# Input gate times cell gate on GpSimd in the last slot of a graph and LSTM kernel

## What is computed

```python
def _L1_gnn_ref(x, adj, Wg0, bg0, Wg1, bg1, Wih, Whh, bih, bhh):
    h = jax.nn.relu(jnp.einsum('ts,bsh->bth', adj, x @ Wg0 + bg0))
    h = jax.nn.relu(jnp.einsum('ts,bsh->bth', adj, h @ Wg1 + bg1))
    for p in range(1, MAX_SKIP + 1):
        nw = Tv // p
        wins = h[:, :nw * p, :].reshape(Bv * nw, p, Hd)
        last = _lstm_last(Wih[p - 1], Whh[p - 1], bih[p - 1], bhh[p - 1], wins)
        idx = jnp.arange(nw) * p + (p - 1)
        h = h.at[:, idx, :].set(last.reshape(Bv, nw, Hd))
    return h
```

## Time and profile before

| | us |
|---|---|
| median of three runs | 1012.63 |
| the profiled execution | 1012.88 |
| its span, from the first to the last instruction | 1011.2 |
| TensorE busy in it | 995.4 |
| VectorE busy | 560.3 |
| ScalarE busy | 378.2 |
| GpSimd busy | 19.9 |

### The profile page before, as it was taken

The page is one execution under the profiler, slowest core; times in us unless marked ns, Lnnn a source line. Parts: engine busy times, 40 slices in busy tenths (PEclk is TensorE's granted clock), DMA queues, the critical chain, the costliest instruction groups (busy, mean ns, idle before and its releaser), DMA issues.

```text
span 1011.2 us, 14383 instructions
## 1 busy us (share of the span) xinstructions
PE 995.4 (98%) x5399; PEld 868.7 (86%) x5399; DVE 560.3 (55%) x1308; ACT 378.2 (37%) x702; POOL 19.9 (2%) x22
## 2 busy tenths in 40 slices
PE   9999999999999999999999999999999999999994
PEld 7888998888988889888898889898988989898894
DVE  7342343323334233332375656777777776767987
ACT  7231111222022120131234445445454464545765
POOL 0000000000000000000000000101010010100000
PEclk9999999999999999999999999999999999999998
DMA  9200000000000000000040000000000000000001
GB/s 358 95 1 1 1 1 1 1 1 1 1 0 0 0 0 0 0 0 0 0 166 1 1 1 1 1 1 2 22 1 21 0 21 0 21 2 22 1 1 64
DMA packets 7535, 20.42 MB, mean 20 GB/s; under 512 B 960, under 2 KB 2240, under 8 KB 7488
## 3 DMA queue, kind: packets, MB, share of 16 engines
q1 hardware_dynamic: 7488, 19.81, 5.2%
HBM read 15.61 MB, written 4.19 MB: 20 GB/s over the span
## 4 chain that ended last, share of the span: by engine, by line
PE 95%; DVE 3%; ACT 1%; issue 1%; DVEq 0%; ACTq 0%
PE ps L948 23%; PE ps L646 18%; PE ps L648 18%; PE ps L647 18%; PE ps L856 9%; PE ps L1001 2%; PE ps L1021 2%; PE ps L706 2%; PE ps L686 1%; PE ps L870 1%; PE ps L1063 1%; DVE stats L1323 1%; PE ps L1095 1%; PE ps L1064 0%; PE ps L1066 0%
## 5 line engine op out<-in xcount | busy, mean ns | idle before, releaser
L1306 DVE TENSOR_TENSOR y<-ps,y 128x512 fp32r<-128x512 f32 x46 | 31.8, 691 | 174.2 <-ACT y L1176 174.2
L1176 ACT ACTIVATE y<-ps 128x512 fp32r<-128x512 f32 x46 | 27.5, 598 | 269.3 <-PE ps L648 269.2
L646 PE MATMUL ps<-adj,node 128*128 128x512 f32 x312 | 122.2, 392 | 0.1
L648 PE MATMUL ps<-adj,node 128*128 128x512 f32 x312 | 121.7, 390 | 0.0
L647 PE MATMUL ps<-adj,node 128*128 128x512 f32 x312 | 121.6, 390 | 0.0
L646 PE MATMUL ps<-adj,h 128*128 128x512 f32 x256 | 99.7, 389 | 0.0
L647 PE MATMUL ps<-adj,h 128*128 128x512 f32 x256 | 99.7, 389 | 0.0
L648 PE MATMUL ps<-adj,h 128*128 128x512 f32 x256 | 99.6, 389 | 0.0
L1309 DVE SCALAR_TENSOR_TENSOR h<-ps,h 128x512 fp32r<-128x512 f32 x112 | 76.2, 688 | 40.0 <-ACT h L1176 39.4
L856 PE MATMUL ps<-s,adj 128*128 128x256 f32 x768 | 93.7, 283 | 0.0
L856 PEld LDWEIGHTS ps<-s,adj 128*128 128x128 f32 x768 | 92.9, 192 | 0.3
(11 more groups left out here) (214 smaller groups left out, 1690.2 us busy)
## 6 DMA issues: line engine op xcount, KB each, us to landing
square<-in_adj_t SPq DMA_DIRECT2D x8, 512.0 KB, 8.9
xb<-in_x SPq DMA_DIRECT2D x8, 512.0 KB, 11.0
adj_raw<-in_adj_t SPq DMA_DIRECT2D x8, 512.0 KB, 7.5
out<-xb SPq DMA_DIRECT2D x7, 512.0 KB, 2.7
lw_raw<-in_wih_t SPq DMA_DIRECT2D x1, 1024.0 KB, 12.4
lw_raw<-in_whh_t SPq DMA_DIRECT2D x1, 768.0 KB, 11.0
w_raw<-in_w SPq DMA_DIRECT2D x1, 512.0 KB, 11.6
out<-xb SPq DMA_DIRECT2D x1, 384.0 KB, 2.9
```

What stands on the lines that cost most here:

```text
L646: pe.matmul(dst, stat(HI), mov(HI), start=start, stop=False)
L648: return pe.matmul(dst, stat(LO), mov(HI), start=False, stop=stop)
L1176: nc.scalar.activation(dst, ps[:, (j * A_MM + q) % BANKS, :], func).then_inc(a_hi, 1)
L1306: nc.vector.tensor_tensor(dst, src, f32(hi), ALU.subtract).then_inc(done, 1)
```

## The change

In slot 8, from step 7 on, every step that has a state (12 steps: 7, 8, 9, 11, 13, 14, 15, 16, 18, 19, 20, 21) has its I * G product issued by GpSimd, in place, after the same wait on `gate_act` that VectorE has. It increments a semaphore of its own, `pool_cell`. VectorE leaves L1593 out there, computes F * c as before, and waits for `pool_cell` ahead of the sum. The counts of `cell_step` that others wait for are lowered to match. Seven of the twelve have 258 elements, four 344, and one (step 8) 512. The rest of the diff, `POOL_ADDS` (empty) and "pool_scale" (in no list), issues nothing. The loop of GpSimd's CASTs for slot 8 keeps its place ahead of step 7's product.

```diff
+        POOL_CELLS = 7
+
+        def pool_cells(slot, k):
+            return slot == B and k >= POOL_CELLS and steps_of(slot)[k].s > 0
...
+            for item in items(B):
+                if isinstance(item, Step) or item == ("end",):
+                    if isinstance(item, Step):
+                        if pool_cells(B, k):
+                            i, g = (gates_in(item.stream)[:, at, span(item)] for at in (GI, GG))
+                            pool.wait_ge(gate_act, AHEAD["gate"][B] + gate + 2)
+                            nc.gpsimd.tensor_tensor(i, i, g, ALU.mult).then_inc(pool_cell, 1)
+                        gate += len(gates_of(item.s))
+                        k += 1
...
-                                nc.vector.tensor_tensor(work(GI), work(GI), work(GG), ALU.mult).then_inc(cell_step, 1)
+                                by_pool = pool_cells(slot, k_step)
+                                if not by_pool:
+                                    nc.vector.tensor_tensor(work(GI), work(GI), work(GG),
+                                                            ALU.mult).then_inc(cell_step, 1)
                                 dve.wait_ge(gate_act, ahead("gate", slot, turn, gate + 3))
                                 nc.vector.tensor_tensor(work(GF), work(GF), work(4), ALU.mult).then_inc(cell_step, 1)
-                                n_cell += 2
+                                n_cell += products(slot, k_step)
                                 step_reached(n_cell)
+                                if by_pool:
+                                    n_pool += 1
+                                    dve.wait_ge(pool_cell, n_pool)
                                 nc.vector.tensor_tensor(work(4), work(GI), work(GF), ALU.add).then_inc(cell_done, 1)
```

More of the change, by code:

```diff
@@ L189, in build @@
         shift_set = sem("shift_set")
+        pool_add = sem("pool_add")
+        pool_cell = sem("pool_cell")
         out_ready = sem("out_ready")
@@ L348, in build @@
                 ("shift", 6, 8, 1), ("scale", 0, 6, 1)]
+        POOL_ADDS = ()
         SLOTS = B + 1
@@ L368, in parts_of @@
         def parts_of(e):
-            return sum(not isinstance(item, Step) and item[0] in ("scale", "shift") and slot - item[3] == e
+            return sum(not isinstance(item, Step) and item[0] in ("scale", "shift", "pool_scale") and slot - item[3] == e
                        for slot, full in ((B - 1, DRAIN), (B, LAST)) for item in full)
@@ L378, in norm_column, with pool_adds, adds_so_far @@
             return NORM_COLUMN.get(e, 0)
+        def pool_adds(slot, item):
+            return slot == B and item[1:] in POOL_ADDS
+        def adds_so_far(slot, n_fin):
+            first = [item for item in items(slot) if item[0] == "fin"][:n_fin]
+            by_pool = sum(pool_adds(slot, item) for item in first)
+            return by_pool, n_fin - by_pool
         def items(slot):
@@ L393, in items @@
                 else:
-                    back = item[-1] if item[0] in ("fin", "stats", "root", "root2", "scale", "shift") else 0
+                    back = item[-1] if item[0] in ("fin", "stats", "root", "root2", "scale", "shift", "pool_scale") else 0
                 if slot < back:
@@ L414, in ends, with products, cell_steps @@
             return u.p == SKIPS and u.s == SKIPS - 1
-        def cell_steps(u):
-            return (2 if u.s > 0 else 0) + (0 if ends(u) else 2)
+        POOL_CELLS = 7
+        def pool_cells(slot, k):
+            return slot == B and k >= POOL_CELLS and steps_of(slot)[k].s > 0
+        def products(slot, k):
+            return 0 if steps_of(slot)[k].s == 0 else 1 if pool_cells(slot, k) else 2
+        def cell_steps(slot, k):
+            return products(slot, k) + (0 if ends(steps_of(slot)[k]) else 2)
         def high_counts(slot):
             n, begun, counts = 0, [], []
-            for u in steps_of(slot):
-                n += 2 if u.s > 0 else 0
+            for k, u in enumerate(steps_of(slot)):
+                n += products(slot, k)
                 for v in finished_by(u, begun):
@@ L434, in build @@
             "unit": lambda n: len(steps_of(n)),
-            "cell": lambda n: sum(cell_steps(u) for u in steps_of(n)),
+            "cell": lambda n: sum(cell_steps(n, k) for k in range(len(steps_of(n)))),
             "fin": lambda n: count(n, "fin"),
@@ L627, in _, with first_half_of_runs @@
             back = 1
-            for slot in range(back, SLOTS):
+            def first_half_of_runs(slot):
                 steps = steps_of(slot)
@@ L639, in _ @@
                 last.then_inc(runs_set, 1)
+                return ready
+            for slot in range(back, B):
+                first_half_of_runs(slot)
+            n_fin, n_norm, gate, k, begun, n_ended = 0, 0, 0, 0, [], 0
+            runs_from = max(i for i, u in enumerate(steps_of(B)) if u.p == 1 and u.back == back)
+            for item in items(B):
[7 more added lines that the diff above has]
+                        k += 1
+                        ended = len(finished_by(item, begun))
+                    else:
+                        ended = len(begun)
+                        begun.clear()
+                    if n_ended <= runs_from < n_ended + ended:
+                        first_half_of_runs(B)
+                    n_ended += ended
+                elif item[0] == "fin":
+                    _, t0, t1, back = item
+                    if pool_adds(B, item):
+                        pool.wait_ge(fin_mm, AHEAD["fin"][B] + n_fin + 1)
+                        rows = xb[:, B - back, t0:t1, :].rearrange("p t c -> p (t c)")
+                        nc.gpsimd.tensor_tensor(rows, rows, ps[:, GB + n_fin % 2, 0:(t1 - t0) * F],
+                                                ALU.add).then_inc(pool_add, 1)
+                    n_fin += 1
+                elif item[0] == "stats":
+                    n_norm += 2
+                elif item[0] in ("root", "root2"):
+                    n_norm += LN_STEPS - 2
+                elif item[0] == "pool_scale":
+                    _, t0, t1, back = item
+                    pool.wait_ge(ln_step, PAIRS * LN_STEPS + AHEAD["norm"][B] + n_norm)
+                    for t in range(t0, t1):
+                        g = norm_column(B - back) + t
+                        rows = xb[:, B - back, t, :]
+                        last = nc.gpsimd.tensor_scalar(rows, rows, mv[:, g, 0:1], newton[:, 1, g:g + 1],
+                                                       ALU.subtract, ALU.mult)
+                    last.then_inc(rows_ready(B, t0, t1, back), 1)
@@ L1090, in pe_slot @@
                             lo_reached(0)
-                            if n_fin > 1:
-                                pe.wait_ge(fin_add, ahead("fin", slot, turn, n_fin - 1))
+                            by_pool, by_dve = adds_so_far(slot, n_fin - 1) if n_fin > 1 else (0, 0)
+                            if by_pool:
+                                pe.wait_ge(pool_add, by_pool)
+                            if by_dve:
+                                pe.wait_ge(fin_add, ahead("fin", slot, turn, by_dve))
                         for t in range(t0, t1):
@@ L1563, in hi_ready @@
                     dve.wait_ge(b_hi, ahead("lo", slot, turn, B_PRE + n))
-                gate, n_cell, n_fin, n_norm, begun, n_ended = 0, 0, 0, 0, [], 0
+                gate, n_cell, n_fin, n_norm, begun, n_ended, k_step, n_pool = 0, 0, 0, 0, [], 0, 0, 0
                 def in_place(u, g):
@@ L1592, in dve_slot @@
                             else:
-                                nc.vector.tensor_tensor(work(GI), work(GI), work(GG), ALU.mult).then_inc(cell_step, 1)
+                                by_pool = pool_cells(slot, k_step)
+                                if not by_pool:
+                                    nc.vector.tensor_tensor(work(GI), work(GI), work(GG),
+                                                            ALU.mult).then_inc(cell_step, 1)
                                 dve.wait_ge(gate_act, ahead("gate", slot, turn, gate + 3))
                                 nc.vector.tensor_tensor(work(GF), work(GF), work(4), ALU.mult).then_inc(cell_step, 1)
-                                n_cell += 2
+                                n_cell += products(slot, k_step)
                                 step_reached(n_cell)
+                                if by_pool:
+                                    n_pool += 1
+                                    dve.wait_ge(pool_cell, n_pool)
                                 nc.vector.tensor_tensor(work(4), work(GI), work(GF), ALU.add).then_inc(cell_done, 1)
                             gate += len(gates_of(u.s))
+                            k_step += 1
                             ended = finished_by(u, begun)
@@ L1707, in dve_slot @@
                         _, t0, t1, back = item
+                        if pool_adds(slot, item):
+                            n_fin += 1
+                            continue
```

(6 more changed lines are left out.)

## The result

The changed kernel takes 1015.36 us (median of 12 runs, 1015.09 to 1015.89) against 1012.97 for the kernel before, measured beside it: a ratio of 1.0024 (95% interval 1.0017 to 1.0032), 2.4 us more. One of the 12 runs of the kernel before took 3529.13 us, for a cause that no profile shows, and the ratio goes by the others. The profiled execution took 1015.38 us with a span of 1013.7, 2.5 us over the 1011.2 of before.

The account below looks back on a forecast made before the run. TensorE bounds the kernel, busy 98%, with engine hand-overs setting the end from 974.8 us. Delays of 2.0 + 1.75 + 0.75 = 4.5 us give 1017.4 profiled, 1017.1 median; range 1013.5 to 1019.2.

Parts of the forecast that it names:

- What the product was worth on the path: I * G in slot 8's tail: mostly hidden behind the wait for gate F, removal gains 0.05 to 0.15 us.
- GpSimd's price: Time of one GpSimd product: 0.68, 0.87 and 1.25 us for 258, 344 and 512 elements.
- The turns: VectorE instructions with two SBUF inputs alternate with GpSimd's reads; each GpSimd product charged in full to such VectorE work.
- VectorE keeps its turn: Rival, chance 0.15: GpSimd gets in only where VectorE pauses; 2.9 us slower, 1015.5 us.
- First stretch: Steps 7, 8 and 9, where TensorE is always busy: 0.45 + 0.70 + 0.87 = 2.0 us late.
- Second stretch: Steps 11 to 16: late by 1.2 + 0.68 less 0.1 of play, 1.75 us.
- the lateness handed on: Steps 13 to 15: tanh and gates share ScalarE in order, so delay grows 0.8, 1.1, 1.2 us.
- Third stretch: Steps 17 to 21: step 21's GpSimd product holds up root's small two-input instructions, 0.75 us late.
- waiting between them: Step 21, in root: the rest of the 0.75 us after 0.68 held up, 0.34 saved, 0.3 brought along.
- Hidden after all: Rival, chance 0.16: GpSimd's products end before F is ready at step 8; gain 0.05 to 0.15 us, 1012.5.
- the case of a gain: Whole kernel faster by over 2.0 us: chance 0.03, as the product on the path is 1.7 us altogether.
- Half hidden: Rival, chance 0.07: TensorE's play is larger than the loads suggest; 0.5 to 2 us, around 1013.8.

Follow-up runs that it names:

- the first kernel: Kernel before, VectorE keeping all products, plus twelve same-size GpSimd products of constant tiles that nobody waits for: 1018.71 us against 1013.05, ratio 1.0059.

## Why the prediction was right, and where its sum was off

The direction, the mechanism and the range held: slower, by the two engines taking turns, 1015.4 in 1013.5 to 1019.2. The point, 1017.1, was too high: 4.5 us forecast, 2.4 measured. That it still fell within the range is in part luck: its lower part stood for a cheaper product or for play that hides it, and the products cost slightly more than forecast. By its own working with the measured prices the sum would have been no less than 4.5.

- *What the product was worth on the path.* I had 0.05 to 0.15 us. The kernel with the MEMSET in the product's place is 0.3 us late although VectorE is spared the product, so nothing is to be had with GpSimd beside. The gain with nothing in the way was not measured.
- *GpSimd's price.* 0.68, 0.87 and 1.25 us were forecast, the middle between the CAST's 1.5 ns per element and twice that; 0.74, 0.93 and 1.28 were measured. The slope between 344 and 512 elements here, 0.35 us for 168, is 2.1 ns, and on top of it some 0.2 us are there at all three sizes. The Trainium skill (GPSIMD Engine Reference, section 3.1, Elementwise) gives 2.6 cycles per element; by estimate that is 2.2 ns at its 1.2 GHz, and the trace agrees with it in the slope.
- *The turns.* Shown by the first kernel and the two with MEMSET. They are not for every instruction of VectorE, as I had charged them: the COPY (L1651, now L1729) kept its 0.52 us beside GpSimd's product in step 16. That GpSimd gets in between two VectorE instructions that stand back to back is shown at 960: CAST, then GpSimd, then the low part. The rival that VectorE keeps its turn (1015.5) came nearest to the time, yet its mechanism is not in the trace: under it L1377 at 960.19 would have kept its 0.88 us.
- *The charge for a turn* is the term that was mis-sized. I charged VectorE the whole of GpSimd's duration. Where GpSimd came into busy VectorE work, VectorE lost 0.53 us at step 9 (1.41 for 0.88, GpSimd 1.10), 0.45 at step 14 (L1377 0.97 for 0.52, GpSimd 0.75), 0.49 at step 21 (0.66 for 0.17, GpSimd 0.73): half to two thirds of the recorded duration. The start of GpSimd's instruction lay beside the VectorE instruction then running. And VectorE was let in early: its end less its usual duration gives a start 0.12 to 0.16 us before GpSimd's recorded end in eleven of the twelve steps, and 0.22 in step 9. What GpSimd does in these parts was not tried. The second CAST near 944 us had shown it beforehand: L1595 ended at 946.26, so with 0.42 of its own it began at 945.84, 0.13 before the CAST's end at 945.97. I read it as coming after that end.
- *First stretch.* Forecast 0.45 + 0.70 + 0.87 = 2.0, measured 0.41 + 0.59 + 0.53 = 1.53. Steps 7 and 8 were near; step 9 has the overcharge.
- *Second stretch.* Forecast 1.75, measured 0.74. Here the step that failed is the lateness handed on. My 1.2 us for step 15's sum had some 0.5 of its own (0.87 less 0.43, and 0.07) and so some 0.7 from steps 13 and 14. Before, ScalarE had been idle for 0.57 us ahead of the gates of step 15, and that play took it all up: in the change tanh of step 14 comes 0.51 us later against the slip, and the gates start 1.54 us later than before, which is the first stretch's 1.53 and no more. Only step 15's own F * c (0.38) and step 16's intrusion (0.36) are left. The two rows are ScalarE's of before and of after:

```profile
974.83 0.55 ACT L1244 ACTIVATE gates_last<-ps,lb 128x344 f32<-128x344 f32 x1 [0.57 <-PE ps L948]
```
```profile
975.89 0.42 ACT L1326 ACTIVATE gates<-gates 128x258 f32<-128x258 f32 x1 [1.30 <-DVE gates L1675]
976.37 0.55 ACT L1315 ACTIVATE gates_last<-ps,lb 128x344 f32<-128x344 f32 x1
```

- *Third stretch.* Forecast 0.75, measured 0.28. Some 0.15 us are given back behind the low part's load, which I had not seen. Step 20 then brings 0.28 (I had 0.3), root is held up by 0.49 and not 0.68, and 0.34 is saved behind it; the "waiting between them" that I added had no row, and it was not there.
- *Hidden after all*, 0.16, and the case of a gain fall with the loads at 952, 960 and 982. *Half hidden*, 0.07, was right in one thing: the play ahead of step 15 was larger than I had it, and some 0.7 of the 2.1 us that the sum had too much stood there.

## What to carry to other kernels

An elementwise product can't be moved from VectorE to GpSimd for nothing just because GpSimd is idle: look first at what VectorE does in that moment, since in these runs its two-input instructions stopped for GpSimd's reads, and 12 products of 0.73 to 1.28 us cost 2.4 us of a chain that they were to relieve. What stood beside VectorE's products for nothing was GpSimd work that only writes; 12 copies still cost 2.2 us. And before crediting a removed instruction that stands in the chain, ask for which operand its successor waits: I * G stood four times in the chain, but by the gates' times F came just as late.

## What the runs showed of the hardware that I had not expected

A CAST of VectorE was held up even by a GpSimd MEMSET (0.77 us for 0.34), while two-input products beside the same MEMSETs kept their time. The Trainium skill (SBUF — State Buffer, Who interferes with whom) has a two-input instruction contend only with GpSimd's reads, and copies and casts, in a mode that uses two ports, with GpSimd in general; the runs agree with the first, and the held-up CAST fits the second, though no row names its mode. It also says that the loser blocks until the other is through; here, by the working above, VectorE's product began 0.14 us before GpSimd's recorded end, so a sum that charges recorded durations comes out too high. And a hand-over by semaphore from GpSimd to VectorE cost 0.27 us more in step 8 than being held up did in the same place.
